# Moving head splits, decoder loads and the output weight's preparation around the attention units of a two-layer float32 transformer kernel

## The reference

```python
q = (x @ wq).reshape(b, s, NH, HD)
k = (x @ wk).reshape(b, s, NKV, HD)
v = (x @ wv).reshape(b, s, NKV, HD)
scores = jnp.einsum('bihd,bjhd->bhij', q, k) * SCALE
attn = jax.nn.softmax(jnp.where(causal, scores, min), axis=-1)
out = jnp.einsum('bhij,bjhd->bihd', attn, v)
...
x = x + ga * (out.reshape(b, s, NH * HD) @ wo)
...
_dequant(codes, scales)          # w = NF4[codes] * scales, in layer 1
```

## Time and profile before

| | us |
|---|---|
| median of 3 runs | 1100.01 (1099.08 to 1101.44) |
| the profiled execution | 1101.38 |
| its span, first to last instruction | 1099.6 |
| PE busy in the span | 953.8 (87%) |
| DVE busy | 703.6 (64%) |
| ACT busy | 537.1 (49%) |
| POOL busy | 203.1 (18%) |
| mean granted clock of PE | 0.925 of full |

### The profile page before, as it was taken

The page is one execution under the profiler, slowest core; times in us unless marked ns, Lnnn a source line. Parts: engine busy times, 40 slices in busy tenths (PEclk is TensorE's granted clock), DMA queues, the critical chain, the costliest instruction groups (busy, mean ns, idle before and its releaser), DMA issues.

```text
span 1099.6 us, 14014 instructions
## 1 busy us (share of the span) xinstructions
PE 953.8 (87%) x5376; PEld 730.5 (66%) x5376; DVE 703.6 (64%) x877; ACT 537.1 (49%) x689; POOL 203.1 (18%) x200
## 2 busy tenths in 40 slices
PE   3793998987778579689899999999996999998996
PEld 1462565655445458577688888868885888886885
DVE  4632789875665667865775666535877867676652
ACT  1411556654443333354376555535772866665640
POOL 2000555554435621600000000000003000000003
PEclk9697899998887879879999999997998999998999
DMA  9276366563312021301053223212330233332202
GB/s 332 85 221 113 45 105 109 66 116 62 47 40 71 24 77 39 74 3 39 19 168 101 86 86 106 79 37 58 96 113 23 80 112 92 100 96 58 77 1 77
DMA packets 40019, 91.62 MB, mean 83 GB/s; under 512 B 6928, under 2 KB 10128, under 8 KB 39952
## 3 DMA queue, kind: packets, MB, share of 16 engines
q1 hardware_dynamic: 35072, 83.66, 30.6%
q10 hardware_dynamic: 4880, 7.07, 2.0%
HBM read 76.02 MB, written 2.10 MB: 71 GB/s over the span
## 4 chain that ended last, share of the span: by engine, by line
PE 58%; DVE 6%; issue 2%; ACT 2%; POOL 2%; POOLq 0%; ACTq 0%; DVEq 0%
PE PS L1370 12%; PE PS L1371 12%; PE PS L1372 12%; PE PS L1653 5%; PE PS L1654 5%; PE PS L1655 5%; PE PS L1573 1%; PE PS L1574 1%; POOL X L610 1%; PE PS L1639 1%; PE PS L1411 1%; DVE XN L996 1%; DVE SCR L1038 1%; PE PS L1629 1%; DVE ST L981 1%
## 5 line engine op out<-in xcount | busy, mean ns | idle before, releaser
L735 ACT ACTIVATE PL<-CODE 128x1024 f32<-128x1024 int32 x200 | 201.5, 1053 | 59.9 <-DVE ACC L1055 41.0
L1370 PE MATMUL PS<-HH,WRH 128*128 128x512 f32 x448 | 174.5, 390 | 0.0
L1372 PE MATMUL PS<-HL,WRH 128*128 128x512 f32 x448 | 174.3, 389 | 0.0
L1371 PE MATMUL PS<-HH,WRL 128*128 128x512 f32 x448 | 174.3, 389 | 0.0
L610 POOL TENSOR_TENSOR X<-X,SCR 128x512 f32<-128x512 f32 x32 | 42.7, 1342 | 663.4 <-DVE SCR L1038 663.2
L774 ACT ACTIVATE PT<-PS 128x512 f32<-128x512 f32 x160 | 86.0, 602 | 95.5 <-PE PS L1487 75.1
L1472 PE MATMUL PS<-KS,QS 128*128 128x128 f32 (+3 forms) x256 | 91.1, 437 | 47.2 <-DVE MX L1167 45.7
L1055 DVE SCALAR_TENSOR_TENSOR ACC<-PL,ACC 128x1024 f32<-128x1024 f32 x100 | 124.8, 1248 | 9.7 <-ACT PL L735 1.5
L626 POOL TENSOR_TENSOR QS<-ident,MX 64x256 fp32r<-64x256 f32 x128 | 94.7, 740 | 112.8 <-DVE MX L1167 106.0
L1167 DVE TENSOR_REDUCE MX<-PS 128x2 f32<-128x256 f32 (+3 forms) x128 | 99.9, 818 | 21.9 <-PE PS L1474 14.2
L1318 DVE TENSOR_TENSOR HID<-SG,PS 128x512 f32<-128x512 f32 x56 | 38.2, 684 | 112.6 <-PE PS L1574 67.6
(11 more groups left out here) (228 smaller groups left out, 1702.1 us busy)
## 6 DMA issues: line engine op xcount, KB each, us to landing
CODE<-in_CODES SPq DMA_DIRECT2D x50, 512.0 KB, 3.6
SCALE<-in_SCALES SPq DMA_DIRECT2D x100, 256.0 KB, 4.3
WM<-in_WM SPq DMA_DIRECT2D x12, 1024.0 KB, 7.0
QS<-FH SPq DMA_DIRECT2D x32, 128.0 KB, 4.1
QS<-FL SPq DMA_DIRECT2D x32, 128.0 KB, 5.2
X<-in_X ACTq DMA_DIRECT2D x2, 1024.0 KB, 12.1
out_x<-X ACTq DMA_DIRECT2D x8, 256.0 KB, 2.0
WF<-in_LBGU SPq DMA_DIRECT2D x14, 128.0 KB, 2.1
```

The source lines that it names most:

```text
L735: nc.scalar.activation(PL[:, n % 3], CODE[:, p % 2], ACT.Prelu, scale=scale, bias=bias, alpha=alpha).then_inc(s_plane, 1)
L1370: nc.tensor.matmul(dst, lh, rh, start=start and k == 0, stop=False)
L1371: nc.tensor.matmul(dst, ll, rh, start=False, stop=False)
L1372: ins = nc.tensor.matmul(dst, lh, rl, start=False, stop=stop and k == KC - 1)
```

## The change

The numbers in the tables are unit numbers (keys of `ROUND_AT`, `SPLIT_AT`) or stack numbers (keys of `PIECES_AT`). The hunks stand in the file's order: tables, buffers, then the queues of POOL, ACT, DVE and PE.

```diff
-PIECES_AT = {2: (0, 1), 5: (2,), 7: (3,), 10: (4,), 12: (5,)}
+PIECES_AT = {0: (0, 1), 5: (2,), 7: (3,), 10: (4,), 12: (5,)}
-SPLIT_AT = {40: 0, 44: 1, 48: 2, 52: 3, 58: 4, 60: 5, 62: 6}
+ROUND_AT = {41: 0, 46: 1, 49: 2, 54: 3, 58: 4, 60: 5, 62: 6}
+SPLIT_AT = {46: 0, 51: 1, 54: 2, 59: 3}
...
-        BTF = sb("BTF", [P, KC, D], F32, dec0 + 16 * K)
-        WOH = sb("WOH", [P, KC, D], F32R, R0 + 48 * K)
-        WOL = sb("WOL", [P, KC, D], F32R, R0 + 56 * K)
+        BTF = sb("BTF", [P, KC, D], F32, dec0 + 24 * K)
+        WOH = sb("WOH", [P, KC, D], F32R, dec0 + 16 * K)
+        WOL = sb("WOL", [P, KC, D], F32R, R0 + 92 * K)
...
-            pool.wait_ge(s_w0h, 1)
-            nc.gpsimd.tensor_tensor(WOL[:], WOF[:], WOH[:], ALU.subtract).then_inc(s_w0l, 1)
...
-                if n in SPLIT_AT:
-                    round_heads(*divmod(SPLIT_AT[n], PAIRS))
-            act.wait_ge(s_wo, 16 * REP)
-            act.wait_ge(s_pv, B * GROUPS * TB)
-            nc.scalar.activation(WOH[:], WOF[:], ACT.Copy).then_inc(s_w0h, 1)
+                if n in ROUND_AT:
+                    round_heads(*divmod(ROUND_AT[n], PAIRS))
+                if n == units - 2:
+                    act.wait_ge(s_wo, 16 * REP)
+                    nc.scalar.activation(WOH[:], WOF[:], ACT.Copy).then_inc(s_w0h, 1)
             round_heads(B - 1, PAIRS - 1)
-            act.dma_start(LDA[:], a["LDA"]).then_inc(s_ldw, 16)
...
             act.wait_ge(s_mm, J["wo", NT - 1] + 1)
+            act.dma_start(LDA[:], a["LDA"]).then_inc(s_ldw, 16)
...
-                if n - 1 in SPLIT_AT:
-                    split_heads(SPLIT_AT[n - 1])
+                if n in SPLIT_AT:
+                    split_heads(SPLIT_AT[n])
 
             last = B * PAIRS - 1
+            dve.wait_ge(s_st, STC(B * GROUPS - 1))
+            dve.wait_ge(s_w0h, 1)
+            nc.vector.tensor_tensor(WOL[:], WOF[:], WOH[:], ALU.subtract).then_inc(s_w0l, 1)
+            for pair in range(PAIRS, last):
+                split_heads(pair)
             copy_odd(last)
+            gates("ga0")
             swap_sums(last)
...
             split_heads(last)
-            gates("ga0")
...
-            pe.wait_ge(s_odd, 2 * B * PAIRS)
...
+                if bank(("wo", t)) == 7:
+                    pe.wait_ge(s_odd, 2 * B * PAIRS)
```

More of the change, by code:

```diff
@@ L767, in _ @@
             done = 0
-            for n in range(B * GROUPS * TB):
+            units = B * GROUPS * TB
+            for n in range(units):
                 ic = n % TB
```

## The result

| | before | after |
|---|---|---|
| median of the runs taken together, us | 1100.13 (1099.08 to 1101.44) | 1051.55 (1049.61 to 1053.67) |
| the profiled execution | 1101.38 | 1050.38 |
| its span | 1099.6 | 1048.5 |
| mean granted clock of PE | 0.925 | 0.954 |

The ratio is 0.9558, with a 95% interval from 0.9535 to 0.9582. The forecast was 1052.5 us, a ratio of 0.957. The size of the whole was right; of its three terms the first was right, the second 0.8 us too high and the third 2.0 us too low.

A forecast was written before the change was run, and what follows sets the result against it. Bound by the wait for `CODE` at attention's start, DVE's queue in the units and a chain at the end; 14.4 + 28.7 + 4.4 = 47.5 off 1101.38 gives 1053.9, less 1.4 to the median: 1052.5 us, range 1047 to 1061.

The forecast's parts named there:

- Piece loads: Start of attention: pieces loaded behind stack 0 let the first `curve_sum` start at about 93.8 instead of 108.23; gain 14.4 us.
- rival A: Start of attention: stacks 1 and 2 arrive late behind the pieces; price 5 us, total 1057.5; chance 0.10.
- Splits and roundings: Attention loop: splits five units behind their rounding make DVE's waits vanish; 21.9 plus 6.8, together 28.7 us.
- Three undisturbed stretches are 73.3: Units 34 to 58: 95.82 us before would become three 24.44 us stretches, 73.3, plus 0.6 for splits; gain 21.9.
- rival B: Loop: rounding and splitting fall on the path, DVE's stretches from unit 34 exceeding 25.5 us; price 5.6, 1058; chance 0.12.
- wrong at the root: Sign: a stretch of eight units past unit 34 can't keep 24.4 us for a reason the earlier waits had hidden.
- The end: From unit 63's maxima through the eight products: earlier `WOH`, `WOL` on DVE, earlier gates; gain 4.4 us, between 2.3 and 7.3.
- Rival C: End of attention: late exponentials, `WOL` and splits make the products wait; the 4.4 becomes -1, total 1058; chance 0.10.
- Contention with GpSimd: Behind `WOL`: splits may meet POOL's scaling, up to 0.7 us each, last split up to 2 us later; sum stays.
- The rest: POOL's last scaling and the experts' weight loads come earlier, but nobody waited for them; nothing gained.
- D: Start of attention: first stall stays because SP's wait or the queue holds `CODE` back; price 14.4 us, 1067; chance 0.04.
- E: Unit 62: ACT waits for `WOF`, delaying unit 63's exponentials; costs once landing takes 14 us longer; slower overall; chance 0.01.

The follow-up runs named there:

- run with other units: Kernel after with pair 1's split moved from unit 51 to 49 and pair 3's from 59 to 62: 1048.61 us, ratio 0.9539.
- kernel with `WOL` behind the diagonal: Kernel after with `WOH` rounded behind unit 59 and DVE waiting for POOL's last diagonal ahead of `WOL`: 1049.81 us, ratio 0.9554.
- The edits alone: Kernel before with only the end new (`WOH` inside unit 62, `WOL` on DVE, gates early without PE's wait for the last sums): 1095.23 us, ratio 0.9959.
- The loop without stalls: Kernel before with only the rounding and splitting tables of the kernel after: 1071.91 us, ratio 0.9758.
- kernel with both edits: Kernel after with splits moved from units 51 and 59 to 49 and 62, and `WOH` rounded behind unit 59: 1051.32 us, ratio 0.9554.

## Why the prediction was right, step by step

**Piece loads, 14.4 forecast, 14.55 measured.** The working held at each step: the issue (78.57, expected at 80.2), curves behind `GR` alone, two of them ahead of the `curve_sum`. Only the six issues were set a little long, at 3.7 us where six times 0.58 is 3.5 and the trace has 3.3; nothing hangs on it. The forecast times, 91.7 and 93.8, came out as 90.03 and 92.06, because GR itself was 1.6 us early. The 5 us kept in the range for late stacks (rival A) weren't needed: unit 4's scores wait for maxima.

**Splits and roundings, 28.7 forecast, 27.9 measured.** That the waits vanish, and that the clock and the pace come back with them, was right. Three sizes inside it were off:
- "Three undisturbed stretches are 73.3" took 24.44 us for units 34 to 42. It is 25.19 in every kernel without a wait there, before any split. So 0.75 us of this stretch was its own, taken for a part of the wait of before. The cause is open. Compared with the stretch before it POOL is busier (17.27 us against 10.53) and the transfers move more (106 GB/s against 73), but the row of units 42 to 50 has as much of both, 17.27 us and 107 GB/s, and takes 24.4 us with a split in it. What sets this stretch apart is the place of its `curve_sum`s, behind the maxima of units 39 and 41 with none between, and a wait of 1.27 us for the scores of unit 41; no run moved them.
- Units 50 to 58 took 25.67 us instead of 25.04. Of these 0.63 us, 0.23 is a third `curve_sum` (units 18 to 26 have three as well and take 24.67, not 24.44). The two splits cost 1.0 instead of 0.6: unit 51's and 54's took 1.38 and 0.98 us instead of 0.69. The run with other units puts 0.5 us on unit 51's.
- Unit 59's split was set at 0.6 and cost under 0.1, so that unit 58 to 63 took 13.42 instead of 14.0. Unit 46's cost nothing, as forecast (24.43).

In the sum 0.75 + 0.63 - 0.58 = 0.8 us, which is the miss. By the prediction's own signs it was not clean: the copies of the sums stand up to 25.67 us apart, over its 25.1 and over the 25.5 that it gave as the sign of rival B, and the sign "wrong at the root", a stretch that can't keep 24.4 us for a reason of its own, came true with 0.75 us. The mechanism stood, at sizes far below B's 5.6 us: at most 0.5 us is left for the roundings.

**The end, 4.4 forecast, 6.4 measured, within its bounds of 2.3 to 7.3.** The mis-sized part is what comes ahead of the first product: 5.15 us, where 2.3 was worked out from the edits and up to 1.9 more allowed for the clock. The first product was set at +13.5 and came at +10.6. Two steps account for the 2.8 us between:
- The exponentials of unit 63 were set at +7.9 and start at +5.7 (291.03 less 285.30), so the gates start at +8.7 and not at +10.7. Without `WOH` in their way they start at +4.5 (in the kernel with `WOL` behind the diagonal, 292.72 less 288.21), so `WOH` costs 1.2 us, not 1.9, and the old +6.0 held 1.5 us more. In the kernel before DVE had just waited 4.49 us for the split at 326.02, and PE stood at a mean clock of 0.52 from 327 to 334; the rows don't part these two.
- The gates were set at 2.78 us and took 1.98, at full clock. In the kernel before the clock fell to 0.50, the 1.2 GHz level, while they ran.

In the products it was the other way round: up to 3.1 us was allowed and 1.24 came. PE reached them at full clock and then stood at 0.50 from 297 to 300 us; in the kernel before it had 0.50 from 341 to 351, some 6 us of it in the products. The edits alone gave 3.1 in the same way, the first product 1.9 us earlier and the eight products in 23.5 us instead of 24.8. The loop without stalls gave 2.2 without any edit at the end, and both together 1.1 more. Rival C (PE waits in the products, or the products catch DVE) did not come: DVE takes product 0 at 305.53, +20.2, and PE is busy without a gap from the first product to 319.46.

The prediction also misread the row of 341 to 344: it puts the 0.50 behind some 7 us in which PE did next to nothing. Ahead of the gates PE idled for 1.58 us, and the clock was still at 0.97 in the first us of the gates (340 to 341) and at 0.50 in the next.

That 6.4 lies inside the bounds is partly luck. In two kernels with the same order at the end (pieces behind stack 1, roundings two units ahead) the products ran at full clock, in 21.9 us, and the stage ended at +32.5: a gain of 8.0, over the 7.3.

The Trainium skill ("TensorE: Matmul & The Clock Gate", What's actually happening) was read in the prediction as giving 7.3, a full clock to the end, and the row of 0.50 as giving 2.3. Neither reading is what the trace shows: the end was denser and the gates ran at full clock, but the first 4.1 us of the products of the kernel after (columns as before) run at a mean clock of 0.62, those of the kernel with `WOL` behind the diagonal at full clock.

```profile
295.90:300.00 4.10, 4.10 (x12) 3.20 (x12) 3.99 (x8) 0.00 (x0) 3.88 (x3) 0.62 0.00 0
```

```profile
297.60:301.70 4.10, 4.10 (x19) 3.41 (x19) 3.99 (x6) 0.00 (x0) 3.71 (x3) 1.00 0.00 0
```

**Contention with GpSimd.** The prediction let the splits meet POOL's scaling and said that the sum would stay. It did: the three splits behind `WOL` took 2.96 us, the last of them beside POOL's scaling, and 1.88 in the kernel with `WOL` behind the diagonal, where POOL scales after them. That cost nothing at the products. Inside the loop it cost 0.5 us in unit 51, where the prediction's bound of 0.69 for a split had left it out. The Trainium skill ("GPSIMD Engine Reference", Specifications) names this contention without a size; the sizes here are 1.38 for 0.69 us on DVE, and 3.54 for 1.30 us on POOL.

**The rest.** Nothing was expected and 0.7 us measured, which is within what this stage varies by (726.3 to 730.3 in the runs here). Rivals D and E did not occur: `CODE` was there, and ACT had no wait for `WOF`.

That the total came within 1 us of the median owes something to chance: the end's +2.0 and the loop's -0.8 partly cancel, and where the products meet the low clock is a matter of 1.6 us. The 1.6 us ahead of GR and 0.7 in the rest are in the span of the profiled execution.

## What to carry over

- Where one engine makes something that another consumes in strict order, the consumer's place in its queue should lie behind the producer's by more units than the consumer runs ahead; here DVE waited up to 6.4 us at one unit, up to 3.0 at two (in two of four splits) and not at all at three and five. A stall cost up to half as much again as the wait itself, with a lower clock in its stretch.
- A stretch that serves as the undisturbed pace should be one that carries the same side work; count what else the stalled stretches hold (here the number and the places of the `curve_sum`s) before taking the pace of their neighbours.
- An instruction brought forward on VectorE can slow the step that everyone waits for on GpSimd, though neither waits for the other; place it behind that step.

## What the runs showed of the hardware that wasn't expected

**VectorE can hold a GpSimd instruction until its own ends.** Two diagonals of 64x256 took 3.54 us beside a VectorE subtraction of two 128x2048 tensors in SBUF and 1.30 us when VectorE was idle, with the one wait as the only edit between the two kernels. Taken one by one it is not a factor on both: the first diagonal took 2.52 us (287.50 to 290.02) instead of 0.61 and ended 0.47 us behind the subtraction (287.27 to 289.55). In the kernel with both edits it is the same, 287.62 to 290.14 with the subtraction ending at 289.67. The second took 0.94 beside the splits that follow. It goes the other way as well: unit 51's split started 0.46 us into a scaling on POOL (250.26 to 251.54), took 1.38 us and ended 0.56 us behind it. I had counted on VectorE alone being slowed.

**With the same queues the granted clock fell in one kernel and not in the other.** These are the same units in the kernel with `WOL` on GpSimd and in the kernel after (columns as before). Their queues up to there are the same, the first only runs some 0.8 us later.

```profile
260.00:262.00 2.00, 1.94 (x11) 0.91 (x9) 1.97 (x4) 2.00 (x4) 1.71 (x2) 1.00 0.97 106
262.00:264.00 2.00, 0.55 (x4) 0.45 (x4) 2.00 (x3) 2.00 (x4) 0.16 (x1) 1.00 0.66 80
264.00:266.00 2.00, 1.99 (x8) 1.01 (x8) 2.00 (x4) 1.78 (x3) 1.83 (x2) 0.72 0.25 53
266.00:268.00 2.00, 2.00 (x28) 1.42 (x27) 1.32 (x1) 1.94 (x4) 1.84 (x3) 0.50 0.17 37
```

```profile
260.00:262.00 2.00, 1.13 (x6) 0.41 (x4) 2.00 (x3) 2.00 (x4) 1.27 (x2) 1.00 0.94 103
262.00:264.00 2.00, 1.36 (x10) 1.21 (x11) 2.00 (x3) 1.95 (x4) 0.71 (x1) 1.00 0.41 68
264.00:266.00 2.00, 2.00 (x32) 1.23 (x31) 2.00 (x4) 1.82 (x4) 1.84 (x3) 1.00 0.23 49
```

In the four us from 260 to 264 PE was busy 2.49 us in both, with 1.03 us as its longest gap in both, yet the clock fell to 0.50, the 1.2 GHz level, in the first and stayed full in the second; the stretch from unit 50 to 58 then took 27.17 us instead of 25.67. The kernel with `WOL` behind the diagonal shows the same fall at the same place (27.19), the other five traces with these queues in the loop don't. The same happens at the products: with the same order there (but for the engine of `WOL` in one) and the first product at +10.63 to +10.65 in each, their end came at +34.2 in three traces and at +32.5 in two. The row of one of the two, the kernel with the pieces behind stack 1, stands against the row of 0.62 above:

```profile
300.00:304.10 4.10, 4.10 (x19) 3.38 (x19) 3.99 (x8) 0.00 (x0) 3.88 (x3) 1.00 0.00 0
```

It makes a term of some 1.5 us for each such place in this kernel that no order of the queues explains, and it is as large as what the last edits here were meant to bring. What decides between the two outcomes is open.
